# Second attention: one head in four is masked by a product on GpSimd instead of a bias on TensorE

## The reference

```
query = layernorm(ctx @ Wq + bq), key, value = layernorm(x' @ Wk + bk), layernorm(x' @ Wv + bv)   # by head: 16 heads of 16
scores = query . key / sqrt(16)                     # 8 x 16 x 512 x 512
scores = where(mask == 0, -1e9, scores)             # one mask for the 16 heads of a batch
out    = softmax(scores) @ value @ Wo + bo
```

## Time and profile before

| what | value |
|---|---|
| median of 3 runs | 2155.09 us (2154.49 to 2155.93) |
| profiled execution, its own time | 2156.33 us |
| its span (first to last instruction) | 2154.6 us |
| second attention's 128 units | about 645 to 1385 us |
| PE busy over the span | 89% |
| DVE, ACT, POOL busy over the span | 74%, 50%, 43% |

### The profile page before, as it was taken

How to read it: one execution, slowest core, us unless ns; L and a number is a source line. 1 busy time by engine, 2 the same in 40 slices (tenths; PEclk the granted TensorE clock), 3 DMA queues, 4 the chain that set the end, 5 groups by cost and what they waited for, 6 DMA issues and landing times. The chain is left out here.

```text
span 2154.6 us, 35704 instructions
## 1 busy us (share of the span) xinstructions
PE 1913.3 (89%) x11904; PEld 1347.0 (63%) x11968; DVE 1601.9 (74%) x3393; ACT 1069.0 (50%) x2062; POOL 919.2 (43%) x682
## 2 busy tenths in 40 slices
PE   5889898987669999999999999919999999999998
PEld 2566666665323343343434343419999999999998
DVE  7999999997546667767776778436777777777775
ACT  2233334433326655555555555415656555556663
POOL 6988888884533334343534331111222222222222
PEclk8899999998859999999999999958999999999999
DMA  5222222220243251515142441045766666666661
GB/s 169 109 89 87 109 86 89 87 94 1 61 100 87 63 123 45 128 45 123 65 110 93 89 121 33 21 146 171 227 225 214 219 225 219 219 228 227 224 209 59
DMA packets 140065, 271.45 MB, mean 126 GB/s; under 512 B 13915, under 2 KB 91823, under 8 KB 134066
## 3 DMA queue, kind: packets, MB, share of 16 engines
q1 hardware_dynamic: 128812, 244.55, 36.7%
q0 software_dynamic: 10624, 25.26, 3.2%
q10 hardware_dynamic: 518, 0.27, 0.0%
HBM read 201.96 MB, written 71.39 MB: 127 GB/s over the span
## 5 line engine op out<-in xcount | busy, mean ns | idle before, releaser
L1434 DVE CUSTOM_DVE_ANT_0 x_dump<-x_ps,x_bias_q 128x512 bf16<-128x512 f32 x512 | 353.2, 690 | 100.6 <-PE x_ps L1127 87.9
L1303 ACT ACTIVATE x_PT<-x_ps 128x512 f32<-128x512 f32 x512 | 292.2, 601 | 225.7 <-PE x_ps L1142 222.6
L1819 POOL DMA_INDIRECT out_dram<-e_y,e_label x78 | 78.9, 1011 | 369.4 <-DVE e_y L1971 357.5
L1915 ACT ACTIVATE X<-m_ps 128x256 f32<-128x256 f32 x312 | 119.1, 382 | 232.6 <-PE m_ps L1852 232.6
L1127 PE MATMUL x_ps<-x_KS,x_QS 96*128 96x512 bf16 x512 | 201.3, 395 | 23.3 <-DVE x_mx L1434 22.6
L1142 PE MATMUL x_ps<-x_QS,x_KS 98*128 98x512 bf16 x512 | 195.7, 382 | 6.7 <-issue 2.6
L1954 DVE TENSOR_TENSOR X<-X,m_ps 128x256 f32<-128x256 f32 x312 | 120.9, 418 | 103.5 <-ACT X L1915 98.9
L1852 PE MATMUL m_ps<-e_x_lo,m_hi 128*128 128x256 f32 x640 | 181.4, 283 | 1.5 <-DVE e_x_lo L1939 1.5
L1852 PE MATMUL m_ps<-e_x_hi,m_lo 128*128 128x256 f32 x640 | 181.3, 283 | 0.0
L1852 PE MATMUL m_ps<-e_x_hi,m_hi 128*128 128x256 f32 x640 | 181.1, 283 | 0.0
L1141 PE MATMUL x_ps<-x_bias_k,x_ident_b 128*128 128x512 bf16 x448 | 171.3, 382 | 1.1 <-issue 1.1
(11 more groups left out here) (301 smaller groups left out, 5409.1 us busy)
## 6 DMA issues: line engine op xcount, KB each, us to landing
m_raw<-in_L_ffn_w_dram SPq DMA_DIRECT2D x117, 1024.0 KB, 5.3
expert_in<-a_blank SPq DMA_DIRECT2D x34, 1032.0 KB, 4.3
parts<-x_part SPq DMA_DIRECT2D x24, 512.0 KB, 3.7
e_x<-expert_in SPq DMA_DIRECT2D x39, 258.0 KB, 4.8
next_mask_k<-in_maskT_dram SPq DMA_DIRECT2D x32, 256.0 KB, 2.6
next_mask_q<-in_mask_dram SPq DMA_DIRECT2D x29, 256.0 KB, 2.8
x_KS<-parts SPq DMA_DIRECT2D x16, 384.0 KB, 11.4
x_QS<-parts SPq DMA_DIRECT2D x8, 576.0 KB, 6.6
```

Of the source, the lines that this page charges most:

```text
L1303: act.activation(PT[unit % 2][:, k, :], ps_st[e % 3], ACT.Exp, scale=DH ** -0.5).then_inc(exp_done, 1)
L1434: dve.tensor_tensor_reduce(out=dump[:, :], in0=ps_max[m % 2], in1=bias_q[b % 2][:, q, :], scale=1.0, scalar=NEG, op0=ALU.add, op1=ALU.max, ...
L1915: act.activation(silu[f % 2], ps_h[f % 4][:, 0:BLK], ACT.Silu).then_inc(silu_done, 1)
```

## The change

For head k = 0 of each unit PE no longer adds the bias: the scores start their bank themselves. After ACT's exponential, POOL caps the 128x512 exponentials at 2^20 and multiplies them in place with a table `keep` (1 where the mask lets a key through, 2^-120 where not), and `values` on PE waits for that product. The table is made by POOL from `bias_k`, four quarters a batch, in units u = 13, 14, 15 and 0. In POOL's order the new work stands behind the deviations and ahead of the scatters and masks. To make room for `keep` three small buffers go: `ones_b` becomes one column read as if repeated, `lower` is written over `L`, and DVE's row maximum writes its unused full-size result back over its PSUM input and not into the SBUF tile `dump`.

```diff
+HIDDEN = 2.0 ** -120
+LIMIT = 2.0 ** 20
+HIDDEN_BY_PRODUCT = 1
...
-        dump = sb("dump", [P, SEQ], BF16)
+        keep = sb("keep", [P, TPB, SEQ], BF16)
...
+            def keep_of(b, j):
+                pool.wait_ge(k_masked, TPB * b + j + 1)
+                wait(pool, p_masked, UNITS * (b - 1) + UNITS - TPB + j + 1)
+                pool.tensor_scalar(keep[:, j, :], bias_k[b % 2][:, j, :], 0.0, HIDDEN, ALU.is_equal, ALU.max).then_inc(keep_done, 1)
+
+            def mask_exponentials(unit):
+                b, u = divmod(unit, UNITS)
+                kc = u % TPB
+                p = PT[unit % 2][:, 0, :]
+                pool.wait_ge(exp_done, 4 * unit + 1)
+                pool.tensor_scalar(p, p, LIMIT, None, ALU.min).then_inc(p_limited, 1)
+                pool.wait_ge(keep_done, TPB * b + kc + 1)
+                pool.wait_ge(p_limited, unit + 1)
+                pool.tensor_tensor(p, p, keep[:, kc, :], ALU.mult).then_inc(p_masked, 1)
...
                     x_deviations(1)
+                if 0 <= unit < NUNITS:
+                    mask_exponentials(unit)
+                b, j = divmod(unit + 3, UNITS)
+                if j < TPB and 0 <= b < BATCH:
+                    keep_of(b, j)
                 if step_of(unit, 5) is not None:
...
-                if u == 0 and k == 0:
+                if u == 0 and k == HIDDEN_BY_PRODUCT:
                     pe.wait_ge(k_masked, TPB * (b + 1))
...
-                pe.matmul(ps_st[e % 3], ident_b[:, :], bias_k[b % 2][:, kc, :], start=True, stop=False)
+                if k >= HIDDEN_BY_PRODUCT:
+                    pe.matmul(ps_st[e % 3], ident_b[:, :], bias_k[b % 2][:, kc, :], start=True, stop=False)
                 pe.matmul(ps_st[e % 3], KS[b % 2][:, h, kc * P:(kc + 1) * P], QS[b % 2][0:HROWS + MROWS, h, :],
-                          start=False, stop=True).then_inc(st_ready, 1)
+                          start=k < HIDDEN_BY_PRODUCT, stop=True).then_inc(st_ready, 1)
...
                 pe.wait_ge(exp_done, 4 * (unit + 1))
+                pe.wait_ge(p_masked, unit + 1)
...
-                dve.tensor_tensor_reduce(out=dump[:, :], in0=ps_max[m % 2], in1=bias_q[b % 2][:, q, :], scale=1.0,
+                dve.tensor_tensor_reduce(out=ps_max[m % 2], in0=ps_max[m % 2], in1=bias_q[b % 2][:, q, :], scale=1.0,
```

More of the change, by code:

```diff
@@ L809, in cross_attention @@
         xT = sb("xT", [P, 2, KC, P])
-        before_b, ones_b = sb("before_b", [P, P], BF16), sb("ones_b", [P, P], BF16)
+        before_b, one_b = sb("before_b", [P, P], BF16), sb("one_b", [P, 1], BF16)
+        ones_b = one_b[:, :].broadcast_to([P, P])
         iota_i, token = sb("iota_i", [P, NE], I32), sb("token", [P, NT], I32)
@@ L813, in cross_attention @@
         table = lambda n, d=F32: sb(n, [P, TPB, NE], d)
-        L, lower, key, one1, one2, tmp = table("L"), table("lower"), table("key"), table("one1"), table("one2"), table("tmp")
+        L, key, one1, one2, tmp = table("L"), table("key"), table("one1"), table("one2"), table("tmp")
         cnt = table("cnt", BF16)
@@ L853, in cross_attention @@
         q_masked, k_masked = sem("q_masked"), sem("k_masked")
+        keep_done, p_limited, p_masked = sem("keep_done"), sem("p_limited"), sem("p_masked")
         kv_ps, kv_var, kv_shift, kv_used = (sem(n) for n in ("kv_ps", "kv_var", "kv_shift", "kv_used"))
@@ L988, in constants @@
                     pool.memset(r32[:, odd, :, :, (1 - odd) * DH:(2 - odd) * DH], 0.0).then_inc(consts, 1)
-                pool.memset(ones_b[:, :], 1.0).then_inc(consts, 1)
+                pool.memset(one_b[:, :], 1.0).then_inc(consts, 1)
                 pool.iota(iota_i[:, :], pattern=[[1, NE]], base=0, channel_multiplier=0).then_inc(tables, 1)
@@ L992, in constants @@
                 pool.wait_ge(consts, 16)
-                pool.affine_select(out=before_b[:, :], in_=ones_b[:, :], compare_op=ALU.is_gt, fill=0.0,
+                pool.affine_select(out=before_b[:, :], in_=ones_b, compare_op=ALU.is_gt, fill=0.0,
                                    base=0, pattern=[[1, P]], channel_multiplier=-1).then_inc(consts, 1)
@@ L1204, in bank_m @@
                     pe.matmul(ps_m[:, 0:TPB * NE], before_b[:, :], counts, start=True, stop=True)
-                    mm = pe.matmul(ps_m[:, TPB * NE:2 * TPB * NE], ones_b[:, :], counts, start=True, stop=True)
+                    mm = pe.matmul(ps_m[:, TPB * NE:2 * TPB * NE], ones_b, counts, start=True, stop=True)
                 else:
@@ L1524, in gate_second @@
             def gate_second(b):
-                do(dve.scalar_tensor_tensor(out=lower[:, :, :], in0=one1[:, :, :], scalar=-3.0e38, in1=L[:, :, :], op0=ALU.mult, op1=ALU.add))
-                best(lower, m2, i2, one2)
+                do(dve.scalar_tensor_tensor(out=L[:, :, :], in0=one1[:, :, :], scalar=-3.0e38, in1=L[:, :, :], op0=ALU.mult, op1=ALU.add))
+                best(L, m2, i2, one2)
             def gate_counts(b):
```

## The result

The changed kernel takes 2275.4 us (median of 4 runs, 2273.1 to 2280.3), the kernel before 2154.8 on the same chips (4 runs, 2151.7 to 2155.9): ratio 1.0569, 95% interval 1.0547 to 1.0591. It is 5.7% slower. The sign was forecast, the size was not: 120 us were lost where 39 were expected, and the time lies outside the range.

What follows compares the result with a forecast made beforehand. PE was taken to set the pace, with POOL's answers late at batch boundaries. The profiled 2156.3 us + 48.3 (boundaries) - 9.3 (PE spared) = 2195.3, forecast as 2194 us, 1.8% slower; range 2143 to 2240.

Steps and rivals of the forecast that it cites:

- What bounds the kernel: In the 128 units PE, 94% busy, sets the pace; POOL, 37% busy, matters by when it answers.
- PE is spared: One 128x512 bias matmul per unit goes: 27.8 us of PE work, the most the change can bring.
- half of it on the path: Two units of four pass PE's saving on: 13.9 us reach the end, before losses at the boundaries.
- The boundary: Units u = 13 to 1, keep_of meets scatters, POOL answers late: 7.6 us at each of six, 45.6 us.
- 4(X + K) - 9.6: Loss per boundary in us; X is a unit's limit and product (2.3), K one keep_of table instruction (2.0), with gaps.
- the range's dear side: Rival, chance 0.16: POOL's limit costs as much as the mask's tensor_scalar, 1.95 us, X = 3.25; total 2240 us.
- The end of batch 0: Boundary without scatters: POOL's lateness costs 1.1 + 1.6 = 2.7 us.
- The other units hold: Away from the boundaries POOL's new work fits the time between its deviations, so nothing is lost there.
- POOL slows DVE: Rival, chance 0.06: DVE's SBUF-to-SBUF tensor_scalars slow beside POOL; 26 us at most, half on the path; 2207 us.
- The maximum to PSUM: DVE's row maximum writing to PSUM: put at nothing; at 0.06 us each, 31 us of DVE, 15 on the path.
- The values' wait: PE's new wait for POOL's product before values is covered, as values run behind the next unit's scores.
- The rule against the row: Skill page: one-input POOL work near line rate, 0.43 us plus dispatch; trace row: mask's one-input tensor_scalar 1.95 us, contradicting it.

Runs made afterwards that it cites:

- the power load: Kernel before, plus small POOL powers (128x15, 128x10) taking about as long as limit, product and table, with hardly any SBUF traffic: 2233.9 us, ratio 1.0375.
- the two loads: Kernel before with POOL's load (full tiles), 2275.0 us, and with the power load (small powers), 2233.9 us.
- POOL's load: Kernel before, with POOL also doing limit, product and table at their places on a tile nobody reads: 2275.0 us, ratio 1.0565.
- the table made once: Changed kernel with the keep table made for batch 0 only and used for all batches: 2226.0 us, ratio 1.0336.
- the products alone: Changed kernel without the limit and with the keep table made by ScalarE, leaving POOL 128 products as new work: 2196.4 us, ratio 1.0209.

## Why the prediction was wrong

**What bounds the kernel** was right: PE sets the pace, and POOL matters by when it answers.

**PE is spared** 27.8 us was right, **half of it on the path** was not: 9 us, a third.

**The boundary**, 4(X + K) - 9.6, was right in kind and place: the intervals grew by 10.0 us, ACT's two waits for POOL grew, and the power load shows it with DVE undisturbed. Two of its terms were off, and against each other. The limit took 1.50 us in place of 1.0, which the range's dear side (1.95) held, so a boundary cost 10.0 in place of 7.6. And the count was five, not six: at the end of batch 6 keep_of meets the scatters too, but no deviations follow. Together 50.3 us in place of 45.6; that they came so near is partly luck. The end of batch 0 lost 3.2 + 2.7 = 5.9 in place of 2.7. Before it came 5.5 us at u = 11 to 13 that I had nothing for, with PE's wait of 3.40 us for a transfer into QS and a clock of 0.50 after it. PE has that wait with the power load too (3.7 us), so POOL's time is enough for it; what made the transfer late was not tried.

**"The other units hold"** is the step that failed. They were put at nothing and lost 67.3 us: 9.8 in the batch of the table, and 12.5 in the last 28 units, where POOL has no deviations to give. The step compared POOL's time with POOL's room and left out what POOL does to DVE while it works; by the two loads that is 40.8 us. The other 21 us are POOL's time after all. A rival had the mechanism, **POOL slows DVE**, with a row in hand (819 in place of 406 ns; it was the second of the four, at 976.88), and sized it at 13 us, 26 at most. Three things in its sizing were wrong. It took eight instructions a batch to be exposed; DVE's lines gained 48 us together (mean after less mean before, times the count, over all its lines but the maximum), most of it on the copy of the inverted sums (11 us), the two splits of the maxima (12 us) and XN (7 us). It took 0.4 us for a meeting; an instruction that meets one of POOL's two-input instructions stands to its end, up to 0.98 us longer, and two in a row are caught by two POOL instructions in a row. And it took half of DVE's loss for the path; but these instructions stand ahead of the maxima, so PE waited 2.64 us where DVE had lost 1.8, and then ran at half clock.

**The maximum to PSUM** was put at nothing in the sum, with 15 us named as what it might cost; it cost 11.

**The values' wait** was called covered. It was not everywhere: PE waited 14.3 us in 15 pieces. Two of them are in the last 28 units, 3.23 us at 1436.8, where keep_of and the scatters put POOL behind, and 3.64 us before the very last values, and there the changed kernel loses 4.2 us more than POOL's load, which has no such wait. Over the whole kernel the load without that wait costs the same, so the wait is not what made the time miss.

**The rule against the row.** The estimate from the Trainium skill's "GPSIMD Engine Reference", section 4.1, was 0.43 us plus dispatch for each one-input instruction. Measured are 1.50 us for one operation on f32 and 1.94 us for the table: the row was right and the page does not hold here; the limit, too, lies above the 1.16 us of the two-input product.

The sum from measured terms: 50.3 + 5.9 (boundaries) + 67.3 (other units) are 123.4 us, but for rounding, in the units. What PE was spared (9 us) and the PSUM write (11) stand inside these. Outside the units 3.8 us went the other way, which makes the 119.6 between the two profiled executions.

No version that masks every head beats the kernel before. The best of those that keep a product on POOL loses 2.1%, without its limit, and the most that PE could give back is 0.4%.

## What to carry to other kernels

An engine's idle share is room only if its neighbours don't notice how it is used. Before work goes to GpSimd, list the DVE instructions that copy from SBUF to SBUF or read two SBUF inputs, see what is queued behind each, and price a meeting with a two-input instruction of GpSimd at the rest of that instruction, not at a slowdown of some per cent. Count at how many places the engine's answers are really awaited. And price a pause of TensorE at more than its length, where the trace shows half a clock behind such pauses.

## What the runs showed of the hardware

- GpSimd on 128x512: minimum with a constant, f32, 1.50 us; product of f32 with bf16, 1.16 us; two operations on bf16, 1.94 us. Here one input was not cheaper than two.
- A DVE COPY or TENSOR_SCALAR from SBUF to SBUF, and one with two SBUF inputs, takes up to 0.98 us more (1.39 in place of 0.40, XN) beside GpSimd's two-input instructions on a full tile and at most 0.42 us more beside its limit and its table. A COPY takes nothing more while GpSimd spends 2.75 us on a power of 128x15.
- The same COPY with its input in PSUM takes 0.42 us, undisturbed beside GpSimd.
- Reading the accumulator behind a 128x512 maximum takes 141 ns when the maximum's full output goes to PSUM, 83 ns when it goes to SBUF.
- In the changed kernel, after a wait of PE of 2.64 us, and after 4 us with 0.02 us busy (988 to 992 us), the granted clock was 0.50 in the next 4 us; with the table made once, after a wait of 2.57 us, it was 0.57 from 838 to 842 us. In the run with the products alone, around a wait of 0.47 us, it stayed at 1.00.
